# A linear-attention and feed-forward layer on one core: the attention loop unrolled, start and seam re-ordered

## What is computed

```python
def _layernorm(x, axis=-1, eps=1e-05): ...
# attention, 16 heads of 32
q, k = silu(x @ Wq), silu(x @ Wk);  v = x @ Wv
q, k = rotate(q), rotate(k)
# in chunks of 128 rows, state S of each head
scores = einsum('bthd,bshd->bhts', qi, ki) * D[None]
o = scores @ vi + (qi * decay_q) @ S
S_new = lam_C * S + (ki * decay_k)^T @ vi
gate = x @ Wg1 @ Wg2
o = group_rmsnorm(o * sigmoid(gate)) * weight
return o @ Wo
...
# feed-forward, 4096 hidden, weights of 4-bit codes with a scale for 32
gate = einsum('th,nh->tn', xt, Wg);  up = einsum('th,nh->tn', xt, Wu)
inter = gelu(gate) * up
out = einsum('tn,hn->th', inter, Wd)
...
x = x + attn(_layernorm(x));  x = x + ffn(_layernorm(x))
```

## Time and profile before

| | |
|---|---|
| time, median of 3 runs | 1410.6 us (1410.16 to 1410.66) |
| the profiled execution | 1410.67 us, its span in the profile 1408.8 us |
| PE busy | 1362.9 us, 97% of the span |
| DVE busy | 1054.0 us, 75% |
| ACT busy | 419.1 us, 30% |
| POOL busy | 248.1 us, 18% |

### The profile page before, as it was taken

One profiled execution on the slowest core, in us unless ns is written; L12 is line 12 of the kernel. 1 busy time (PEld: TensorE's weight loads), 2 busy tenths in 40 slices (PEclk: granted clock), 3 DMA queues, 4 the chain that ended last, 5 costly groups with the idle time before them and its releaser, 6 DMA issues.

```text
span 1408.8 us, 18942 instructions
## 1 busy us (share of the span) xinstructions
PE 1362.9 (97%) x7120; PEld 1127.5 (80%) x7120; DVE 1054.0 (75%) x1684; ACT 419.1 (30%) x669; POOL 248.1 (18%) x138
## 2 busy tenths in 40 slices
PE   5799999998899999999999999999999999999998
PEld 4678888886788888888888888888888888888886
DVE  7788878887776867777686868677776768686844
ACT  4334333332322222222222322222222222222221
POOL 3234434333110101011010101010101101011100
PEclk9899999999999999999999999999999999999999
DMA  9000000000010100010010101000000000000002
GB/s 314 23 1 16 2 16 0 15 1 1 1 42 19 30 16 30 16 30 30 15 30 15 30 16 43 15 30 15 30 15 30 30 15 30 15 30 16 1 30 90
DMA packets 21760, 40.20 MB, mean 29 GB/s; under 512 B 2644, under 2 KB 2900, under 8 KB 21588
## 3 DMA queue, kind: packets, MB, share of 16 engines
q1 hardware_dynamic: 20624, 39.08, 8.6%
q10 hardware_dynamic: 1092, 0.53, 0.2%
HBM read 35.40 MB, written 4.19 MB: 28 GB/s over the span
## 4 chain that ended last, share of the span: by engine, by line
PE 91%; DVE 5%; issue 1%; DMA 1%; ACT 1%; SPq 0%; DVEq 0%; ACTq 0%
PE bank L918 28%; PE bank L919 28%; PE bank L920 28%; PE bank L932 2%; PE bank L1001 1%; PE bank L1018 1%; PE bank L1107 1%; DMA w_in<-wk_dram 1%; PE bank L1008 1%; PE bank L1029 1%; DVE x1l L741 0%; DVE bst L505 0%; PE bank L968 0%; PE bank L967 0%; DVE nt_t L498 0%
## 5 line engine op out<-in xcount | busy, mean ns | idle before, releaser
L918 PE MATMUL bank<-x1h,wh 128*128 128x512 f32 x1024 | 398.7, 389 | 0.0
L920 PE MATMUL bank<-x1h,wl 128*128 128x512 f32 x1024 | 398.5, 389 | 0.0
L919 PE MATMUL bank<-x1l,wh 128*128 128x512 f32 x1024 | 398.5, 389 | 0.0
L851 POOL TENSOR_TENSOR wl<-wf,wh 128x1024 fp32r<-128x1024 f32 (+1 forms) x48 | 114.9, 2395 | 853.2 <-ACT wh L375 853.2
L918 PEld LDWEIGHTS bank<-x1h,wh 128*128 128x128 f32 x1024 | 192.4, 188 | 40.0
L920 PEld LDWEIGHTS bank<-x1h,wl 128*128 128x128 f32 x1024 | 192.2, 188 | 39.9
L919 PEld LDWEIGHTS bank<-x1l,wh 128*128 128x128 f32 x1024 | 192.2, 188 | 39.8
L778 DVE SCALAR_TENSOR_TENSOR hx<-hx,bank 128x512 f32<-128x512 f32 x128 | 88.0, 688 | 154.8 <-ACT hx L453 154.8
L918 PE MATMUL bank<-wh,hh 128*128 128x512 f32 x512 | 200.2, 391 | 3.2 <-DVE x1l L741 3.2
L919 PE MATMUL bank<-wl,hh 128*128 128x512 f32 x512 | 200.0, 391 | 0.0
L920 PE MATMUL bank<-wh,hl 128*128 128x512 f32 x512 | 199.9, 390 | 0.0
(11 more groups left out here) (108 smaller groups left out, 1490.5 us busy)
## 6 DMA issues: line engine op xcount, KB each, us to landing
pk<-packed_dram SPq DMA_DIRECT2D x48, 256.0 KB
sc<-scales_dram SPq DMA_DIRECT2D x48, 256.0 KB
out_dram<-acc SPq DMA_DIRECT2D x16, 256.0 KB, 2.2
acc<-x_dram SPq DMA_DIRECT2D x3, 1024.0 KB, 14.1
w_in<-wq_dram SPq DMA_DIRECT2D x2, 512.0 KB, 4.6
w_in<-wk_dram SPq DMA_DIRECT2D x2, 512.0 KB, 10.0
w_in<-wv_dram SPq DMA_DIRECT2D x2, 512.0 KB, 14.6
maskT<-mask_dram SPq DMA_DIRECT2D x1, 1024.0 KB, 11.7
```

What stands on the lines that cost most here:

```text
L851: nc.gpsimd.tensor_tensor(wl[par][:, bass.ds(u, 1), :].rearrange("p a w -> p (a w)"), wf[:].rearrange("p a w -> p (a w)"), wh[par][:, bass ...
L918: pe.matmul(dst, w_h, x_h, start=start, stop=False)
L919: pe.matmul(dst, w_h, x_l, start=False, stop=False)
L920: return pe.matmul(dst, w_l, x_h, start=False, stop=stop)
```

## The change

1. The loop over sequences 1 and 2 is written out; tile numbers are then constants in all of `tile`.
2. Start: PE does four products of zeros (`st`, plain float32) into a bank that nobody reads, ahead of the first transpose of x, and two behind it. Tiles 0 and 1 of x are loaded and normalised first, tiles 2 and 3 come behind Wv. Wg1, Wg2, `rot` and `norm_w` go through SP's queue. The low part of Wv is DVE's, and the transpose of x of tile 1 has a bank of its own, ahead of the v product of tile 0. `silu_qk(1)` and `gate_low(1)` stand ahead of tile 0, `stats` of sequences 2 and 3 are spread over tiles 1 and 2 in pieces of two, `stats_r` of them is in tile 3, and `wo_hi` and `wo_lo` come earlier.
3. The unpacking of units 0 to 2 begins in tiles 4, 6, 8, is scaled in 5, 7, 9 and split in 6, 8, 10 (before: 2, 6, 10; 3, 7, 11; 4, 8, 12).
4. `stats2` is in three pieces: rows of tiles 0 to 7 in tile 11, 8 to 11 in tile 13, ahead of `gated`; the rest in step 0. Tiles 0 to 3 of x1 are transposed in tile 14, 4 and 5 in tile 15, the gate and up products of step 0, half 0, are in tile 15.

```diff
+LN2_ROWS = (0, 8, 12, 16)
+UNIT_BITS, UNIT_SCALE, UNIT_PARTS = (4, 6, 8), (5, 7, 9), (6, 8, 10)
...
-        BX = [bank[n] for n in (1, 6, 1, 6, 5, 6, 5, 6, 5, 6, 7, 6, 4, 5, 6, 7)]
+        BX = [bank[n] for n in (0, 6, 0, 1, 5, 6, 5, 6, 5, 6, 7, 6, 4, 5, 6, 7)]
...
-            for c in range(CHUNKS):
-                body(0, c)
-            with eng.Fori(1, BATCH - 1) as b:
-                for c in range(CHUNKS):
+            for b in range(BATCH):
+                for c in range(CHUNKS - (b == BATCH - 1)):
                     body(b, c)
-            for c in range(CHUNKS - 1):
-                body(BATCH - 1, c)
             last_tile()
...
+                if t in (1, 2):
+                    dve.wait_ge(s_x[t + 1], 16)
+                    stats(4 * t + 4, 4 * t + 6)
...
+                if at_start(b, c):
+                    wo_lo()
+                if t in (1, 2):
+                    stats(4 * t + 6, 4 * t + 8)
+                if t == 3:
+                    stats_r(2 * CHUNKS, TILES, 2)
+                if t == 11:
+                    stats2(0)
+                if t == 13:
+                    stats2(1)
...
+            pe.wait_ge(s_st0, 1)
+            for n in range(4):
+                pe.matmul(BO[:], st[:, 0, :], st[:].rearrange("p k t -> p (k t)"), start=True,
+                          stop=True)
             pe.wait_ge(s_id, 16)
             x_transpose(0)
+            for n in range(2):
+                pe.matmul(BO[:], st[:, 0, :], st[:].rearrange("p k t -> p (k t)"), start=True,
+                          stop=True)
...
                 if not near_end(b, c, 2):
                     x_transpose(t + 2)
+                else:
+                    pe.wait_ge(qk_silu, t + 2)
+                    x1_transpose(0, 0)
+                    pe.wait_ge(v_sb, t + 2)
+                    x1_transpose(1, 0)
...
+                else:
+                    x1_transpose(2, 1)
+                    pe.wait_ge(x1_done, t)
+                    x1_transpose(3, 0)
...
-                pe.wait_ge(st_done, kvs(BATCH - 1, c))
-                x1_transpose(0, 0)
-                pe.wait_ge(v_sb, t + 1)
-                x1_transpose(1, 0)
+                pe.wait_ge(dq_lo, UP + 1)
+                pe.wait_ge(x1t_lo, 4)
+                gate(0, 0, 0)
                 o_transpose(t - 1)
...
-                x1_transpose(3, 2)
                 inter()
+                up(0, 0, 0)
                 intra(t, c)
+                x1_transpose(4, 4)
                 o_back(t)
+                pe.wait_ge(x1_done, t)
+                x1_transpose(5, 4)
...
-                if at == 0:
-                    pe.wait_ge(x1_done, TILES - 1)
-
-                    x1_transpose(4, 4)
-                    x1_transpose(5, 4)
-                gate_up(q, par_q, tb, 0)
+                if at != 0:
+                    gate_up(q, par_q, tb, 0)
+                    down(s - 1, par_q if tb else 1 - par_q, 1)
+                gate_up(q, par_q, tb, 1)
                 if at == 0:
                     o_transpose(TILES - 1)
                     x1_transpose(6, 5)
                     x1_transpose(7, 6)
-                else:
-                    down(s - 1, par_q if tb else 1 - par_q, 1)
-                gate_up(q, par_q, tb, 1)
-                if at == 0:
                     x1_transpose(8, 7)
                     x1_transpose(9, 8)
                     o_ready(TILES - 1)
```

More of the change, by code:

```diff
@@ L180, in build @@
         s_r2 = sem("s_r2")
-        s_vlo = sem("s_vlo")
         s_st0 = sem("s_st0")
@@ L330, in xt_hi_ @@
                 act.wait_ge(v_ps, t)
-                A(xth[:], BV[:].rearrange("p (k t) -> p k t", k=KT), ACT.Copy).then_inc(xt_hi, 1)
+                src = BO if isinstance(t, int) and t == 1 else BV
+                A(xth[:], src[:].rearrange("p (k t) -> p k t", k=KT), ACT.Copy).then_inc(xt_hi, 1)
             def gate_low(t):
@@ L412, in tile @@
                     xt_hi_(t + 2)
+                else:
+                    x1t_hi_(0)
+                    x1t_hi_(1)
                 if not near_end(b, c, 3):
-                    ahead = (c + 3) // CHUNKS + 1
-                    norm1(t + 3, b + ahead + 1)
-                if at_start(b, c):
-                    wo_hi()
+                    norm1(t + 3, 3 if t + 3 < 2 * CHUNKS else 5)
                 ot_copy(t)
                 square(t)
-                if c == 0 and not (isinstance(b, int) and b == 0):
-                    unit_hi(b - 1, b - 1, 0)
-            def x1t_hi_(t):
-                act.wait_ge(x1t_ps, t + 1)
-                A(x1h[:, t // 4, :, P * (t % 4):P * (t % 4) + P],
-                  BX[t][:].rearrange("p (k t) -> p k t", k=KT), ACT.Copy).then_inc(x1t_hi, 1)
+                if near_end(b, c, 2):
+                    x1t_hi_(2)
+                    x1t_hi_(3)
+                if t in UNIT_PARTS:
+                    unit_hi(UNIT_PARTS.index(t), UNIT_PARTS.index(t), 0)
             def last_tile():
@@ L626, in stats2 @@
             def stats2(n):
-                first, last = (0, TILES - CHUNKS) if n == 0 else (TILES - CHUNKS, TILES)
+                first, last = LN2_ROWS[n], LN2_ROWS[n + 1]
                 rows = slice(first, last)
@@ L633, in stats2 @@
                 dve.wait_ge(ln2_done, last)
-                newton(s_ntl, ln2[:, rows, 1], last - first, r2[:, rows], NT * (4 + n), 1.0,
+                newton(s_ntl, ln2[:, rows, 1], last - first, r2[:, rows], NT * (3 + n), 1.0,
                        LN_EPS)
@@ L813, in step @@
                     x1t_lo_(11)
-                    stats2(1)
+                    stats2(2)
                 if at == 1:
@@ L936, in x_transpose @@
                 pe.wait_ge(xn_done, t + 1)
+                if isinstance(t, int) and t == 1:
+                    transposes(BO, xn).then_inc(xt_ps, 1)
+                    return
                 pe.wait_ge(v_sb, t)
@@ L973, in v_project @@
                 first = isinstance(t, int) and t == 0
-                project(BV, 2, (s_vlo, 1) if first else None).then_inc(v_ps, 1)
+                project(BV, 2, (s_wlo, 5) if first else None).then_inc(v_ps, 1)
             def gate2(t):
@@ L1104, in tile @@
                         pe.wait_ge(xt_lo, t + 3)
+                    else:
+                        pe.wait_ge(x1t_lo, 2)
                     pe.wait_ge(kd_done, kvs(b, c) + 1)
```

201 lines of the change are left out of this document (105 added, 96 removed).

## The result

The changed kernel takes 1396.3 us (median of 4 runs, 1395.0 to 1396.6), the kernel before 1410.6 (4 runs beside it). The ratio is 0.9898, 95% interval 0.988 to 0.9915. The profiled execution took 1396.43 us with a span of 1394.3, 14.5 less than before. The forecast of 1392.0 was 4.3 us too low; the time lies in the range, near its upper end.

What follows compares the result with a forecast made beforehand. PE was taken as the bound, with only waits and half clock at start and seam, and small waits between, to win. 8.4 + 6.3 + 2.3 - 0.9 + 2.6 = 18.7 us off 1410.67 gave 1392.0, range 1387.5 to 1397.5.

Steps and rivals of the forecast that it cites:

- Term A: Start to scores of tile 0: earlier weights and full clock win 8.4 us, bounds 5.0 to 10.5.
- term B: Tile 1: normed(0) follows at once, both PE gaps and half clock behind them go, winning 6.3 us.
- C: Tile 2: both gaps of PE go, winning 2.3 us.
- D: Tiles 3 to 13: POOL's low parts delay DVE in tiles 7, 9 and 11, costing 0.9 us net.
- E: The seam, from tile 14's scores to down's second group: shorter waits win 2.6 us, bounds 0 to 5.
- Rival 1: Start: zeros don't bring full clock, or small tables queued ahead of Wk delay weights; 1396 to 1398 us, chance 0.2.
- Behind 365 us: The remaining 1043 us, the same program in both kernels, stay as they are: 0 us.
- Rival 4: Written-out tiles 4 to 11 aren't loaded in time and PE pauses in each, making the kernel slower; chance 0.03.

Runs made afterwards that it cites:

- e1_g1_alone: The changed kernel with Wg2 counted on a semaphore of its own, so ACT's copy of Wg1 waits for Wg1 alone: 1390.7 us.
- e4_seam: The changed kernel with step 0's up products moved: half 0 behind x1's transpose of tile 5, half 1 between those of tiles 7 and 8: 1391.4 us.
- e6_unrolled_only: The kernel before with only the loop over sequences 1 and 2 written out: 1411.5 us, ratio 1.0006.
- e5_act_queue: The changed kernel with Wg1, Wg2, `rot` and `norm_w` back in ACT's DMA queue: 1392.7 us.
- e9_bunched: The changed kernel with Wo's low part and eight bn_stats again in one piece behind tile 0's state copy, ahead of normed(0): 1402.0 us.

## Why the prediction was right, and where not

The time lies in the range, but not because the sum was right. Term A was 5.1 us too high and the end lost 1.0 that the sum didn't have; B, C and D together brought 2.2 more than forecast, E 0.2 less. Without the 2.2 the time would have been 1398.5 (an estimate, 1396.3 + 2.2), outside the range, and up to 1.5 of it is luck in the clock, as term B and C show below.

**Term A (8.4, measured 3.3)** failed at one step: "The v product ends near 21.4." I had worked out when Wv lands from the bytes ahead of it, but put ACT's work in order of arrival. ACT takes it in the order of the program, and there the copy of Wg1 stood ahead of Wv's high parts, with a wait that also counted Wg2, which the change had put behind Wv in the queue. The rule that the prediction should have followed for each transfer that changes its queue: which wait counts it, and what stands behind that wait. With that wait gone (e1_g1_alone) the v product ended at 21.41 and the q product came at 23.96 against my 24.2. This step is 2.75 us of the 5.1 (26.95 against 24.2). The other 2.3 are a second assumption, "at full clock": behind the wait of 2.5 us the clock fell to half, and from q product to scores it took 13.1 us where the term (24.2 to 35.0) has 10.8. In e4_seam, with the same start at full clock, it took 10.80, and DVE's chain ended last, as forecast. So the chain's length was right, though its parts as written add up to 11.6 and not 11.3; in the changed kernel's trace the slow products, and not that chain, led to the scores.

A single trace gives this term to no better than 2 us: the kernel before has its own half clock at the q product of tile 1, which was counted as won, and the same start in e6_unrolled_only hadn't. A third assumption was wrong without effect: Wk's second half came almost 3 us earlier than I had it, and e5_act_queue shows that this is the queue.

**Rival 1** (0.2) had the right time, 1396 to 1398, and neither of its mechanisms. The zeros did bring full clock to the first products, and Wg1 in SP's queue did not make Wk later. It was right only in that a small table in that queue is what comes late; that was Wg2, behind Wv.

**Term B and C (8.6, measured 10.1).** The mechanism holds: e9_bunched brings both waits back and loses 6.3 to 7.1 us. The size was off by 1.5. "PE's wait for the masks of tile 0 stays" was not quite right: it shrank from 2.77 to 1.97 us, and the products behind it ran at full clock, 1.08 instead of 1.93 us. This is the row at 43.80 above; before it was

```profile
47.90 1.93 PE L1018 MATMUL bank<-pr,vs 128*32 128x128 f32 x32 [2.77 <-DVE pr L687]
```

The shorter wait is the kernel's; it is 1.94 to 1.97 us in every trace with the new start. The full clock behind it is luck: six of the twelve traces with the new start have it, six don't. In e4_seam, which doesn't, B and C come to 9.3 us.

**Term D (-0.9, measured -0.2).** Against e6_unrolled_only, whose unrolled loop alone saves 0.4, it is -0.6, close to the forecast. The small operation of DVE beside POOL's low part takes 2.3 us here as well (2.27 us at 237.26), and PE's waits for it in tiles 7, 9 and 11 are 0.36, 0.54 and 0.37; I had put 1.3 on the second, since I took three bit operations of tile 8 as partly uncovered, and they were covered. The comparison itself was the weaker point: the price of the new places has to be set against the old places in the new order, not in the old one, and there it is a gain of 2.7.

**Term E (2.6, measured 2.4).** Wait for the last `sq` 0.80 and 0.56 (forecast 1.0 and 0.9), third x1 transpose 3.25 (3.3), down 0.95 (1.0 to 1.5), low part of x1's tile 3 1.36 (1.2), and tile 14's waits of 1.6 and 0.45 us are gone, as forecast. Nothing of it had to be revised. What the wait at the third x1 transpose and the slow products behind it cost shows in e4_seam, which nearly removes them and gains 2.8.

**Behind 365 us (0, measured -1.0).** That "the program is the same in both kernels, so I leave the remaining 1043 us as they are" was right for the program and not for the clock. The wait of 2.29 us at 368.83 is also in the kernel before (2.28), but it was followed by fewer slow products there: 0.95 against 0.90 over 35 us. Which of the two a trace gets is luck, as the last section shows.

**Rival 4** (slower, unrolled tiles not loaded in time) is refuted by e6_unrolled_only and by the changed kernel's tiles 4 to 11.

## What to carry to other kernels

When a transfer changes its queue, find every wait that counts it, then everything that stands behind that wait on the waiting engine: a semaphore shared by two transfers makes the early one as late as the late one (3.0 us here at the next product that depends on it). A part of a change that looks like a price against the old order may be what keeps its other parts from colliding: price it in the new order. And a thing worth nothing while another wait ends last (the zeros, beside the wait for Wg2) can be worth 1.9 us as soon as that wait is gone, so it is to be tried again after each such step. Before a gain or a loss of 1 to 3 us in one trace is put down to an edit, the clock behind the waits has to be compared too.
